# The scratch tile of a paced scatter loop shrinks from 512 elements to one

## The reference

```python
x = L0_attn_x
xn = _layernorm(x, axis=-1)
# attention: k, q, v = xn @ W.T + b; softmax(causal(q @ k.T * d**-0.5)) @ v
# experts:   top 2 of softmax(xn @ Wr + br);  h = relu(xn @ W1[e] + b1[e]);  y = h @ W2[e] + b2[e]
out = jnp.einsum('bse,bsem->bsm', gate, y)
x = x + _L0_attn_ref(xn, ...) + _L0_ffn_ref(xn, ...)
```

## Time and profile before

| | |
|---|---|
| median of 3 runs | 219.64 us (218.44 to 221.8) |
| the profiled execution | 219.64 us |
| its span in the profile | 217.8 us |
| mean granted TensorE clock | 0.892 |
| busy share: PE, DVE, ACT, POOL | 80%, 51%, 51%, 46% |

### The profile page before, as it was taken

The page is one execution under the profiler, slowest core; times in us unless marked ns, Lnnn a source line. Parts: engine busy times, 40 slices in busy tenths (PEclk is TensorE's granted clock), DMA queues, the critical chain, the costliest instruction groups (busy, mean ns, idle before and its releaser), DMA issues.

```text
span 217.8 us, 4809 instructions
## 1 busy us (share of the span) xinstructions
PE 173.5 (80%) x1416; PEld 152.7 (70%) x1416; DVE 111.7 (51%) x422; ACT 111.3 (51%) x321; POOL 99.7 (46%) x133
## 2 busy tenths in 40 slices
PE   6879998889897600189999999999998999879700
PEld 6869467467795500089898998989988989846700
DVE  3617985369797710064455434443443434244495
ACT  1882595568987600055685646654564646526100
POOL 7000048888888888101455453544555344550000
PEclk9975799599999975558999999999999999999965
DMA  5999999931111111595010010000000000007433
GB/s 156 303 302 179 396 427 399 409 117 39 39 38 37 40 37 37 162 295 133 19 41 33 18 39 24 8 26 27 37 17 36 14 32 32 16 0 218 170 96 96
DMA packets 22215, 24.74 MB, mean 114 GB/s; under 512 B 2689, under 2 KB 15499, under 8 KB 22064
## 3 DMA queue, kind: packets, MB, share of 16 engines
q1 hardware_dynamic: 19664, 20.20, 29.6%
q0 software_dynamic: 2528, 4.24, 5.6%
HBM read 16.02 MB, written 9.39 MB: 117 GB/s over the span
## 4 chain that ended last, share of the span: by engine, by line
PE 51%; POOL 22%; DVE 9%; issue 7%; ACT 5%; DMA 4%; DVEq 0%; SPq 0%; POOLq 0%; ACTq 0%
PE pO L923 24%; POOL slots_dram L355 14%; POOL tick L357 8%; PE pS L910 6%; PE pS L912 5%; PE pS L911 5%; DVE xin L715 4%; PE pT L903 4%; ACT rows L379 3%; PE pS L756 2%; PE pO L858 2%; PE pO L748 1%; DMA slots<-slots_dram 1%; DMA xin<-in_L_attn_x 1%; DMA slots_dram<-rows,slotrow 1%
## 5 line engine op out<-in xcount | busy, mean ns | idle before, releaser
L923 PE MATMUL pO<-w,xT 128*128 x376 | 82.7, 305 | 2.3 <-ACT xT L461 1.3
L461 ACT ACTIVATE xT<-pS,b1t 128x128 f32<-128x128 f32 x188 | 53.4, 371 | 59.7 <-PE pS L912 52.1
L363 POOL DMA_INDIRECT pairs_dram<-ybuf,pair x47 | 46.2, 983 | 60.9 <-DVE ybuf L689 49.0
L923 PEld LDWEIGHTS pO<-w,xT 128*128 128x128 f32 x376 | 57.0, 193 | 4.0 <-issue 3.5
L355 POOL DMA_INDIRECT slots_dram<-rows,slotrow x32 | 32.0, 999 | 33.0 <-DVE slotrow L551 24.4
L910 PE MATMUL pS<-xT,w1hi 128*128 128x128 f16 x188 | 42.4, 226 | 2.9 <-DVE xT L681 2.0
L680 DVE CAST xT<-pT 128x128 f16<-128x128 f32 x47 | 13.6, 290 | 59.4 <-PE pT L903 54.1
L912 PE MATMUL pS<-xT,w 128*128 128x128 f16 x188 | 42.4, 225 | 0.0
L911 PE MATMUL pS<-xT,w1hi 128*128 128x128 f16 x188 | 42.3, 225 | 0.0
L910 PEld LDWEIGHTS pS<-xT,w1hi 128*128 x188 | 21.6, 115 | 4.9 <-issue 4.9
L903 PE MATMUL pT<-ident,slots 128*128 128x128 f32 x47 | 13.2, 286 | 14.6 <-DMA slots<-slots_dram 14.6
(11 more groups left out here) (117 smaller groups left out, 224.9 us busy)
## 6 DMA issues: line engine op xcount, KB each, us to landing
w<-in_L_ffn_W SPq DMA_DIRECT2D x8, 1024.0 KB, 16.6
slots_dram<-slots SPq DMA_DIRECT2D x1, 2860.0 KB, 13.7
slots<-pairs_dram SPq DMA_DIRECT2D x8, 256.0 KB, 4.7
slots<-slots_dram SPq DMA_DIRECT2D x1, 1495.0 KB, 11.0
xin<-in_L_attn_x SPq DMA_DIRECT2D x4, 256.0 KB, 3.3
b2t<-in_L_ffn_b SPq DMA_DIRECT2D x1, 1024.0 KB, 16.9
out<-xin SPq DMA_DIRECT2D x8, 128.0 KB, 1.8
slots<-slots_dram SPq DMA_DIRECT2D x1, 780.0 KB, 6.6
```

What stands on the lines that cost most here:

```text
L363: pool.indirect_dma_start(pairs_dram, bass.IndirectOffsetOnAxis(ap=pair[:, j:j + 1], axis=0), ybuf[:, j % NYB, :], None, bounds_check=NT * ...
L461: ins = nc.scalar.activation(hid[:, j % NHB, here], pA(j)[:, here], ACT.Relu, bias=b1t[:, c, j:j + 1])
L923: return pe.matmul(pO[r % 2][:, 0:D], hid[:, r % NHB, c * P:(c + 1) * P], w, start=(c == 0), stop=(c == NCH - 1))
```

## The change

`tick`, the tile that GpSimd fills between two scatters, has one element a partition in place of 512. The fill, its semaphore and the wait for it stay, and so do the number and the order of all instructions on every engine. Tiles allocated behind `tick` in SBUF (`slots` and its views) can lie up to 2044 bytes a partition lower.

```diff
@@ -119,7 +119,7 @@
         negm = sb("negm", [P, NT], F32)
         rsum = sb("rsum", [P, NT], F32)
         rinv = sb("rinv", [P, NT], F32)
-        tick = sb("tick", [P, 512], F32)
+        tick = sb("tick", [P, 1], F32)
```

## The result

| | before | changed |
|---|---|---|
| median of 4 runs | 220.11 us (218.44 to 221.8) | 231.42 us (229.69 to 231.9) |
| the profiled execution, its span | 219.64, 217.8 us | 231.85, 230.0 us |

The ratio of the fast executions is 1.0529, with a 95% interval of 1.0476 to 1.0582: slower. The forecast was 206.0.

The account below looks back on a forecast made before the run. The scatter strand was taken to bound the kernel, ending 14.57 us after attention. Shorter fills save 31 x 0.44 = 13.6 us, contention and clock add 0: 219.64 - 13.6 = 206.0 us, range 202.5 to 209.0.

Parts of the forecast that it names:

- What bounds the kernel: Scatter strand beside attention: scatter ends last by 14.57 us, TensorE waiting from 77.07 to 91.64 for the sorted rows.
- 31 x 0.44 = 13.6: GpSimd's fills between scatters: 31 fills each 0.44 us shorter bring the last scatter, and the end, 13.6 us forward.
- Attention ends at 77.07: TensorE's attention strand: its end stays at 77.07, 0.9 us before the rows are transposed at 78.0.
- Nothing is charged: DMA engines while weights load: closer scatters add 0.5 us of load, wanted only in the expert loop; charged 0.
- I charge 0 there: VectorE beside GpSimd: a weight's split takes 0.74 us with or without GpSimd's work, so contention adds 0.
- The prediction's last part: Expected later profile: fills about 100 ns, steps about 1.35 us, wait about 0.9 us; wrong if attention ends after 77.07.
- Attention gets no faster from the shorter fills: VectorE in attention: shorter GpSimd fills do not speed it up despite the shared SBUF port; 0 us.
- The cap: TensorE's wait before the expert loop: a faster scatter by itself can gain at most 14.57 us, giving 205.1.
- Rival 1, the clock: TensorE in the expert loop: clock holds at 2.4 GHz, saving 2.4 us more, 203.6 us; chance 0.2.
- Rival 2, the fill was not the cost: GpSimd's step hardly shrinks: at the extreme 219.6 us, chance 0.04; a costlier fill gives 209.4, chance 0.12.
- Rival 3, pacing: GpSimd held in each scatter until the one before lands: steps 2.39 us, 18 us added, 237.6; chance 0.03.
- The sign: Whole kernel: faster 0.93, same 0.04, slower 0.03.

Follow-up runs that it names:

- e2: Against the kernel before: no fill, semaphore or wait behind a scatter, scatters back to back; 198.87 us where before took 214.73.
- c1: The change word for word, repeated on another chip against the kernel before; 202.25 us beside 215.01, ratio 0.9411.
- e1: Against the kernel before: fill of 256 elements in place of 512, semaphore and wait kept; 207.79 us where before took 214.73.
- d1: The kernel before, unchanged, profiled once more against itself; 215.14 us, ratio 1.0016.
- f1: Against the kernel before: no fill, semaphore or wait behind a scatter, run again in a later group; 199.95 us beside 214.96, ratio 0.9294.
- d2: The change once more against the kernel before, in a later group; 201.81 us, ratio 0.9401.
- f2: The change against the kernel before, timed beside the kernel without a fill; 201.47 us where before took 214.96, ratio 0.9356.
- c3: Against the kernel before: tick keeps 512 elements, only 64 are filled; 203.73 us beside 215.01.
- c4: Against the kernel before: one-element tick filled twice behind each scatter, each with semaphore and wait; 206.89 us beside 215.01.
- g3: Against the kernel before: no fill, no extra loads, tick with 512 elements, at a second-kind place; 232.44 us where before took 220.74.
- g1: Against the kernel before: no fill, 60 small SyncE loads added behind the projections, at a second-kind place; 235.32 us where before took 217.7.
- g2: Against the kernel before: no fill, 60 small SyncE loads added, at another second-kind place; 233.67 us where before took 220.74.

## Why the prediction was wrong

**What bounds the kernel.** Right for the kernel before. The scatter ended last, and at the first kind of place the expert loop's first transpose came 5.3 to 5.4 us after the last scatter was issued whether that was at 71.46 (e2), 73.51 (c1), 80.26 (e1) or 87.4 (d1); in all fifteen traces it was 5.2 to 5.6 us but for f1 with 6.8. In the recorded trace of before it was 5.4.

**The term 31 x 0.44 = 13.6.** Right in size at both kinds of place. The new fill took 0.113 us in place of 0.10, so the saving is 0.539 - 0.113 = 0.426 us a step and 31 x 0.426 = 13.2 in all. At the first kind the stretch from the first scatter to the last got 13.0 to 13.2 us shorter (c1, d2, f2 against d1), and the time fell from 214.9 to 201.8, 13.1 us. That the recorded run issued its last scatter within 0.05 us of the forecast is partly luck: its scatter began at 30.52 in place of 29.86 and took 14.2 us less, as its longest DMA instruction took 1.17 us in place of 1.46. The plain steps of 1.41, 1.50 and 1.57 us (c3, c4, e1) gave 203.7, 206.9 and 207.8, in order.

**"Attention ends at 77.07".** Here it broke. The step that failed is in the part on what happens beside the scatter. It kept the end of attention at 77.07 by charging nothing for closer scatters: "Nothing is charged" for their load on the DMA engines, and "I charge 0 there" for contention, on the ground that one split of a weight took VectorE 0.74 us with and without GpSimd's work. The row was true and looked at the wrong thing. No group of instructions of VectorE, ScalarE or GpSimd got longer by more than 0.03 us on average in attention, and a matmul of a given shape took as long as before at either level of the clock. What got longer was the way from the end of a matmul to the rise of its semaphore, which no row of an engine's durations shows. It put the end of attention 27.0 us later, of which 14.57 were covered by the wait that the scatter had left, so some 12.3 remained. The prediction's last part named this outcome, attention ending later because closer scatters disturb it, and gave it no chance and no price.

**"Attention gets no faster from the shorter fills".** This was wrong too, in the other direction, though it is not what decided the sign. One operation, L599, stood for all of VectorE. Others had been slowed by the long fills, as the timelines of VectorE before and after the change show:

```profile
69.22 0.56 DVE L591 TENSOR_SCALAR expo<-expo 128x4 int32<-128x4 int32 x1
```

```profile
69.09 0.17 DVE L591 TENSOR_SCALAR expo<-expo 128x4 int32<-128x4 int32 x1
```

Before the change a fill ran from 69.22 to 69.75. Of the 16 small operations of L590 to L593 in attention seven took 0.35 to 0.70 us before; in the changed kernel all took 0.17 to 0.24. Four of the seven lie over a fill, the three of 0.70 beside a scatter's DMA instruction. The masking of 128 x 768 scores (L605) took 1.48 us before and 0.96 after. VectorE's busy time from the first scatter to the end of attention was 41.5 us in both traces of before and 36.8 to 37.1 us in the four of the change. At the first kind of place attention ended at 80.0 in the one trace of before and at 73.4, 76.0 and 74.0 in the three of the change; how much of that the shorter fills brought is not told apart from the clock, which also differed. So for these operations the trace shows the sharing that the prediction looked for in L599 alone. The wait that was forecast as 0.9 us was 5.4 in c1.

**The cap.** The 14.57 us was treated as a limit of the gain. It was also the cover that hid any slip of attention; with a faster scatter each us of slip is path. The range's upper end, 209.0, also lay under the prediction's own bound of 219.64 - 10.2 = 209.4.

**Rival 1, the clock.** At the recorded place the clock fell during attention, which TensorE spent largely waiting, so nothing is decided there. That the loop took as long as before is a balance: the clock was low in it for 3.4 us (107.1 to 110.5) in place of 7.6, and ScalarE's waits on "remote" in it (L461) were 8.8 us in place of 6.1. At the first kind the rival was wrong, as the clock did fall behind attention, and the step of the prediction was right in part. Windows of c1 (clock in the third column from the right) show it falling behind the end of attention and coming back inside 85 to 90, 7.7 us after the first transposes, where the prediction had 7.6.

```profile
75.00:80.00 5.00, 0.69 (x2) 0.29 (x2) 0.56 (x3) 0.00 (x0) 0.00 (x0) 0.62 0.68 182
80.00:85.00 5.00, 4.57 (x36) 4.25 (x37) 3.22 (x11) 2.79 (x9) 0.00 (x0) 0.50 1.17 296
85.00:90.00 5.00, 4.82 (x45) 4.54 (x45) 1.92 (x9) 2.90 (x9) 0.18 (x1) 0.85 0.67 165
```

But the wait in c1 was 5.41 us. In the other two traces of the change there the clock came back 5.0 us (d2) and 4.6 us (f2) after the first transposes. In e2, whose wait of 0.59 us is the case that the rival spoke of, the clock fell at 78.5 and was full again at 81.9:

```profile
74.00:78.00 4.00, 1.48 (x10) 0.96 (x9) 2.78 (x11) 0.31 (x1) 0.00 (x0) 1.00 0.80 213
78.00:82.00 4.00, 3.56 (x31) 3.44 (x32) 2.17 (x9) 2.00 (x7) 0.00 (x0) 0.57 1.21 297
```

**Rival 2, the fill was not the cost.** Wrong: the step shrank by all of it.

**Rival 3, pacing.** Its sign came true and its mechanism did not. GpSimd was held nowhere: the median of its scatters was 0.96 us. That is where the prediction looked for harm, so the "two in flight without harm" of the argument against it said nothing about the third party, TensorE. Also, the expert loop's distance of 1.28 us, used as evidence that closeness is harmless, comes in 10 of the loop's 46 steps, whose mean is 2 us, in a trace in which that loop had late raises: the row of 6.1 us on "remote" was there to be read, and so were the missing rises, 341 of 512.

**The sign.** The measured ratio and the forecast are each right for a kind of place. Three timed comparisons at the first kind gave 0.936 to 0.941; the recorded one gave 1.053. What makes a place of the second kind is open. It isn't the number that a chip carries, since runs under one number met both kinds at different times; within a group of runs on one chip the kind never changed. What in the close scatters does the harm there is open too. GpSimd's semaphore raise, the addresses behind `tick` and the exact rhythm are excluded (g3), and landings of small loads alone don't do it (g1 and g2 behind 77 us); that the landings of scatters differ from those of loads, or that GpSimd's issuing of them matters, was not tested. One rival concerns the measurement itself. The late raises come only in traces where many rises are missing (33 to 93% of the scatters', against 3% at most), and every execution here comes with a span and a granted clock, so it seems to have been recorded while it ran. Whether the recording takes part in the hold-up no run here tells.

## What to carry to other kernels

An idle stretch of one strand is also the other strand's cover: before taking it away, ask what hides in it, and look at the waits whose releaser is unknown, for they can mean that a finished instruction's semaphore rose late. A loop that only paces DMAs may be there for a place other than the one in hand: without the fill this kernel takes 199 to 200 us in one kind of place and 232 in the other, with 512 elements 215 and 220. Time a change that packs DMAs closer on more than one chip before believing either sign. And one operation whose duration doesn't change with another engine's work says nothing of the others: compare all groups of the engine.

## What the runs showed of the hardware

TensorE's semaphore raises can come over 20 us after the end of the matmul (22.6 us in g2, from 52.27 to 74.91) while indirect scatters of 128 rows are issued every 1.26 to 1.35 us. The few raises of ScalarE and VectorE that are recorded in the same stretch come within 20 ns. This was so in four runs at places where before takes 217.7 to 220.7 us, and in none of seven profiled runs with the same distances where it takes 214.4 to 215.0, nor in the eight with longer distances there. In the four runs 84 to 93% of the scatters' rises were missing from the trace, in the fifteen 3% at most. Before at the first of these places had 33% missing, late raises in the expert loop and none in attention.

At such a place 60 small loads by SyncE were issued 1.12 us apart during the scatters and 0.5 us apart behind them; at the one other place where this was run they came 0.51 us apart throughout.

With fills of 512 float32 elements a partition on GpSimd, small VectorE operations took up to 0.70 us in place of 0.17, and the masking of 128 x 768 scores 1.48 us in place of 0.96; the split of a 128 x 512 weight stayed at 0.74 us.
